# A fused cross-attention and ternary feed-forward kernel: row shifts on halves of the array, an earlier place for them in a queue, and five smaller edits

## The chip, the cores and the metric

The kernel runs on one core of one Trainium2 chip. The metric is the time of one execution in microseconds (us), as the median of several runs. TensorE (PE) multiplies, VectorE (DVE), ScalarE (ACT) and GpSimd (POOL) work on elements, and the DMA queue of SyncE (SP) moves nearly all data.

## The reference

For x of 64 batches x 64 rows x 256 and a context of 64 x 64 x 64, in float32:

```
h   = layernorm(x)                                  # 256 wide
k   = rope(ctx)                                     # kv_rope, 64 wide
q_r = h @ Wq.T, then per head @ w_kc_q @ W_qr       # 16 heads, 64 wide
k_r = k @ W_kr                                      # per head
a   = softmax(q_r . k_r)                            # over the 64 context rows
c   = a @ k;  x1 = x + (c @ w_kc_kv per head) @ Wo.T
h   = layernorm(x1)
u   = quant(rmsnorm(h)) @ ternary(w1).T             # 256 -> 1024
x2  = x1 + quant(rmsnorm(gelu(u))) @ ternary(w2).T  # 1024 -> 256
```

quant rounds a row to 8-bit steps of its own maximum; ternary rounds a weight matrix to -1, 0, 1 by its mean absolute value.

## The kernel before

**Tiling.** The 4096 rows of x are 32 tiles of 128 rows, two batches each (`NT` = 32, `LAST` = 31). The weights are folded first: `ah`/`al` hold the product that takes the normed x straight to the 16 heads' scores, `bh`/`bl` the product behind the attention; hi and lo halves keep float32 accuracy in three passes.

**Slots.** The main loop runs over slots n = 0 to 30, the same n on every engine, and a hand-written tail follows. In slot n the engines work on different stages of different tiles: scores of tile n, the exponentials of tile n, the division of tile n-2, the output projection of tile n-3, `up` (the first feed-forward matmul) of tile n-5, and `down` (the second) of tile n-7. In odd slots two tiles' `up` and two roundings of x fall due, and two tiles are normed in even ones. Every engine executes its list in the order written; semaphores tie the lists together.

**The softmax.** `quadrant_max` (DVE, two per slot) takes maxima of the scores in the PSUM banks `SB[0]`, `SB[1]`. PE turns them (`turned`, L790), and `row_max` (L1054) writes the negated maxima of a tile into `nmax`. `shift_rows` on the SP queue (L359) sends them with two small DMAs into four partitions of `shift`, which is zero elsewhere. Then `shifts` on PE adds them to the scores: two matmuls per slot (L830), one per batch, with the selecting matrix `em[:, b, :]` (128 rows by 128 columns) as stationary operand and 512 columns of `shift` as moving one. ACT takes the exponentials (L563), PE multiplies by the context (`contexts`, L838), and DVE divides (`divide`, L1074) by row sums that have gone out to DRAM (`rinv_rows`, L367) and come back spread over partitions into `rb` (`rinv_spread`, L376).

**The SP queue.** In slot n its order is: `turn_g(n-7)` (a DMA transpose of the rounded `qb`, L389), `shift_rows(n)`, `rinv_rows(n-1)`, in odd slots `turn_x` of two tiles (DMA transposes of `xq`, L381), `rinv_spread(n-1)`, in slot 1 the load of `w2`, in slot 2 a load of x, and `store(n-8)`. An instruction that waits holds up all behind it.

**DVE.** `reciprocal_deviations` makes 1/sqrt(variance) of a part of the tiles with 12 small operations that wait for one another. Parts 2 and 3 stand in slots 6 and 18 behind `g_scale`, ahead of the quadrant sums of that slot and the quadrant maxima of the next.

**Order of one slot on PE.** `scores`, then in even slots `up` of tile n-5, then `queries`, `turned` and `project` in halves, `queries`, `shifts`, in every fourth slot (2, 6, ... 26) a group of transposes `kv_t` (L744), `contexts(n-1)`, `down(n-7)`, and in odd slots `up(n-5)`. After the loop the tail has its own order.

Of the kernel before, what the change touches and what calls it, by code (L numbers as in the profile page):

```python
# [24 lines left out]
P = 128  # L25
# [9 lines left out]
BB = 4  # L35
# [15 lines left out]
RSQRT_OPS = 9  # L51
RSTD_STEPS = RSQRT_OPS + 3
# [7 lines left out]
def build(nc, x, kv, wq, wk_t, wqr, wkr_t, wkv, wo_t, w1_t, w2_t, consts, out):  # L60
    with ExitStack() as ctx:
# [16 lines left out]
        em = sb("em", [P, 2, P], F32R)  # L78
# [73 lines left out]
        cst = sb("cst", [P, 2 * DC + 3 * P], F32, at)  # L152
# [25 lines left out]
        names += """const_set shift_zeroed t_made t_copied d_made d_copied at_made at_copied a_made a_hi a_lo_done rope_steps rope_done kvt_made  # L178
# [17 lines left out]
        def rsqrt(e, v, y, a, t, out, done, n):  # L196
# [7 lines left out]
            step(e.tensor_scalar(y.bitcast(I32), v.bitcast(I32), -0.5, float(0x5F3759DF), ALU.mult, ALU.add))  # L204
            step(e.scalar_tensor_tensor(out=t, in0=v, scalar=1.0, in1=y, op0=ALU.mult, op1=ALU.mult))
            step(e.scalar_tensor_tensor(out=a, in0=t, scalar=1.0, in1=y, op0=ALU.mult, op1=ALU.mult), False)
            step(e.scalar_tensor_tensor(out=t, in0=t, scalar=1.0, in1=y, op0=ALU.mult, op1=ALU.mult))
            step(e.scalar_tensor_tensor(out=t, in0=t, scalar=-10.0 / 3.0, in1=a, op0=ALU.add, op1=ALU.mult))
            step(e.scalar_tensor_tensor(out=y, in0=t, scalar=5.0, in1=y, op0=ALU.add, op1=ALU.mult))
            step(e.scalar_tensor_tensor(out=t, in0=v, scalar=1.0, in1=y, op0=ALU.mult, op1=ALU.mult))  # L210
            step(e.scalar_tensor_tensor(out=t, in0=t, scalar=1.0, in1=y, op0=ALU.mult, op1=ALU.mult))
            step(e.scalar_tensor_tensor(out=out, in0=t, scalar=-3.0 * CUBIC * CUBIC, in1=y, op0=ALU.add, op1=ALU.mult))
            return n
# [17 lines left out]
        def reciprocal_deviations(dve, part):  # L231
# [6 lines left out]
            at_least(dve, sem["rstd_steps"], n - 1)  # L238
            if part < 2:
                dve.wait_ge(sem["bn_means"], XPARTS[part + 1])  # L240
                dve.tensor_scalar(v, mv[:, c, 1], EPS_LN, None, ALU.add).then_inc(sem["rstd_steps"], 1)
            else:
                dve.wait_ge(sem["x_sums"], 2 * (XPARTS[part + 1] - XPARTS[2]))
                dve.tensor_scalar(v, mv[:, c, 1], 1.0 / D, EPS_LN, ALU.mult, ALU.add).then_inc(sem["rstd_steps"], 1)
            dve.wait_ge(sem["rstd_steps"], n)
            n = rsqrt(dve, v, y, a, t, r, sem["rstd_steps"], n)
            dve.tensor_scalar(rstd[:, c], r, RSQRT_SCALE, None, ALU.mult).then_inc(sem["rstd_steps"], 1)
            dve.wait_ge(sem["rstd_steps"], n + 1)
            dve.scalar_tensor_tensor(out=nmean[:, c], in0=mv[:, c, 0], scalar=-1.0 if part < 2 else 1.0, in1=rstd[:, c], op0=ALU.mult, op1=ALU.mult).then_inc(sem["rstd_steps"], 1)  # L249

        cos_t = cst[:, 0:DC]
        em_c = cst[:, 2 * DC:2 * DC + 2 * P]
        id_c = cst[:, 2 * DC + 2 * P:]
# [10 lines left out]
        def tile(t):  # L264
            return 0 <= t < NT
# [53 lines left out]

        def out_tile(t):  # L320
            return (yo if t < NT - 2 else xn)[:, t % 2, :]
# [29 lines left out]
        with nc.Block() as block:  # L351
            @block.sync
            def _(sp):
                def shift_rows(u):
                    p = u % 2
                    sp.wait_ge(sem["row_maxima"], u + 1)
                    at_least(sp, sem["shifted"], 2 * (u - 1))
                    for gg in range(2):
                        sp.dma_start(shift[BB * gg:BB * gg + 2, p, :].bitcast(F32).rearrange("b (k s) -> b k s", s=32),  # L359
                                     nmax[:, p, 32 * gg:32 * gg + 32].bitcast(F32)).then_inc(sem[f"shift_rows{p}"], 16)  # L360
# [9 lines left out]
                def rinv_spread(u):  # L370
                    p = u % 2
                    sp.wait_ge(sem[f"rinv_stored{p}"], 32 * (u // 2 + 1))
                    at_least(sp, sem["ctx_divided"], 2 * u)
                    for half in range(2):
                        rows = rinv_d[p, :, :, :].rearrange("b g n -> (b g) n")[half:4 - half:3 - 2 * half, :]
                        sp.dma_start(rb[64 * half:64 * half + 64, :, :], rows.partition_broadcast(64)).then_inc(sem["rinv_spread"], 16)  # L376
# [23 lines left out]
                sp.dma_start(cst[:, 0:2 * DC + 2 * P], consts[:, 0:2 * DC + 2 * P]).then_inc(sem["consts_loaded"], 16)  # L400
# [12 lines left out]
                for n in range(LAST):  # L413
                    if tile(n - 7):
                        turn_g(n - 7)
                    shift_rows(n)
                    if tile(n - 1):
                        rinv_rows(n - 1)
                    if n % 2 and tile(n - 5):
                        turn_x(n - 5)  # L420
                        turn_x(n - 4)
                    if tile(n - 1):
                        rinv_spread(n - 1)
                    if n == 1:
                        sp.dma_start(w2_s[:, :, :], w2_t.rearrange("(a p) n -> p a n", p=P)).then_inc(sem["w2_loaded"], 16)
# [12 lines left out]
                rinv_rows(LAST)  # L438
# [23 lines left out]
            def _(pool):  # L462
# [40 lines left out]
                pool.memset(red[:, :, :], 1.0).then_inc(sem["const_set"], 2)  # L503
                pool.wait_ge(sem["rstd_steps"], RSTD_STEPS)
# [43 lines left out]
            def _(act):  # L548
# [55 lines left out]
                def w_sum(k):  # L604

                    w, s = ((w1_s, "w1_loaded"), (w2_s, "w2_loaded"))[k]
                    act.wait_ge(sem[s], 16)
# [132 lines left out]
            def _(pe):  # L740
# [84 lines left out]
                def shifts(u):  # L825
                    if u == 0:
                        pe.wait_ge(sem["shift_zeroed"], 1)
                    pe.wait_ge(sem[f"shift_rows{u % 2}"], 32 * (u // 2 + 1))
                    for b in range(2):
                        pe.matmul(SB[b], em[:, b, :], shift[:, u % 2, :], start=False, stop=True, skip_group_check=True).then_inc(sem["shifted"], 1)  # L830
# [97 lines left out]
                for q in range(4):  # L928
                    if q == 0:
                        pe.wait_ge(sem["consts_loaded"], 32)  # L930
                        pe.wait_ge(sem["const_set"], 5)
# [79 lines left out]
                down(LAST - 6)  # L1011
# [3 lines left out]
                project_high(LAST - 1)  # L1015
                up(LAST - 3, 0)
# [18 lines left out]
            def _(dve):  # L1035
                def quadrant_max(u, b):
                    if b == 0:
                        dve.wait_ge(sem["scores"], u + 1)
                        if u == 0:
                            dve.wait_ge(sem["const_set"], 5)  # L1040
# [28 lines left out]
                def divide(u, b):  # L1069
                    if b == 0:  # L1070
# [4 lines left out]
                                      rb[:, b, :].rearrange("p (h s) -> p h s", s=S), ALU.mult).then_inc(sem["ctx_divided"], 1)  # L1075
# [153 lines left out]
                dve.tensor_copy(em[:, :, :], em_c.rearrange("p (b c) -> p b c", c=P)).then_inc(sem["const_set"], 1)  # L1229
# [16 lines left out]
                for n in range(LAST):  # L1246
                    k = n // 2 + 1
                    if tile(n):
# [21 lines left out]
                    if n % 2 == 0 and tile(n - 6):  # L1270
# [3 lines left out]
                        if n in (6, 18):  # L1274
                            reciprocal_deviations(dve, 2 + n // 18)
# [115 lines left out]
```

## Time and profile before

| | |
|---|---|
| time before, median of 3 runs | 413.43 us (412.06 to 414.34) |
| profiled execution, its time | 413.87 us |
| profiled execution, its span | 412.1 us |
| granted TensorE clock, mean | 0.996 |
| busy: PE, DVE, ACT, POOL | 90%, 76%, 67%, 52% |
| main loop, slots 4 to 29 | about 73 to 354 us of the span |

A row of a timeline gives start, length, engine, line of the kernel, operation, operands, number of instructions, and in brackets the idle time of the engine ahead of it with what ended it. Matmuls overlap in time: a float32r matmul of 256 columns is shown with 0.28 us, and the next starts 0.12 us after it. "SPq" is the issue of a DMA by SyncE, not its transfer.

### The profile page before, as it was taken

How to read it: one execution, taken by the hardware profiler on the slowest of the kernel's cores; microseconds unless marked ns; L12 is line 12 of the kernel's file. 1: busy time of each engine (PE TensorE's matmuls, PEld its weight loads, DVE VectorE, ACT ScalarE, POOL GpSimd, SP SyncE). 2: the span in 40 equal slices, each digit the busy share in tenths (PEclk: the TensorE clock that was granted, in tenths of full speed). 3: DMA queues.
4: the chain of work that ended last, by engine and by line, in shares of the span. 5: the costliest groups of instructions: out<-in, count | busy, mean ns of one | idle time of the engine just before them, and what ended most of it. 6: DMA issues, size and time to landing. Idle time of an engine off the chain costs nothing.

```text
span 412.1 us, 8855 instructions
## 1 busy us (share of the span) xinstructions
PE 371.6 (90%) x2829; PEld 267.3 (65%) x2829; DVE 312.0 (76%) x859; ACT 276.8 (67%) x541; POOL 215.6 (52%) x262
## 2 busy tenths in 40 slices
PE   0978879999899999999999999999999999886775
PEld 0657547667677776767676767777777767544632
DVE  0497656687978687868787988868787878796884
ACT  1253467799786888878777768585848585855771
POOL 1120132792738375756666563827382746594770
PEclk9999998999999999999999999999999999999999
DMA  8999055313344435442525335252444353434446
GB/s 272 365 431 295 18 156 155 79 45 91 46 86 92 106 90 105 92 104 71 123 71 112 84 68 127 42 131 60 109 82 104 93 105 91 105 93 104 103 111 120
DMA packets 63901, 48.81 MB, mean 118 GB/s; under 512 B 50160, under 2 KB 55536, under 8 KB 62704
## 3 DMA queue, kind: packets, MB, share of 16 engines
q1 hardware_dynamic: 63328, 45.50, 45.0%
q10 hardware_dynamic: 528, 2.75, 2.0%
q8 instruction: 23, 0.38, 0.4%
q14 instruction: 22, 0.18, 0.2%
HBM read 31.98 MB, written 4.46 MB: 88 GB/s over the span
## 4 chain that ended last, share of the span: by engine, by line
issue 29%; POOL 26%; PE 20%; DMA 10%; DVE 7%; SPq 4%; ACT 2%; POOLq 1%; ACTq 0%; DVEq 0%
POOL tq L489 6%; POOL cl L466 6%; POOL qb L492 6%; DMA cst<-consts 4%; POOL xa L479 2%; POOL xn L331 2%; PE hps L775 2%; DMA shift<-nmax 2%; PE ps L757 2%; POOL yc L474 2%; PE ps L838 2%; PE ps L759 2%; PE ps L758 2%; DMA qt<-qb 2%; PE hps L848 2%
## 5 line engine op out<-in xcount | busy, mean ns | idle before, releaser
L466 POOL TENSOR_TENSOR cl<-cr,ch 128x512 fp32r<-128x512 f32 x63 | 79.3, 1280 | 111.0 <-ACT ch L568 111.0
L757 PE MATMUL ps<-xh,ah 128*128 128x256 f32 x256 | 74.9, 292 | 1.3 <-DVE xl L348 0.8
L552 ACT ACTIVATE qf<-ps 128x512 f32<-128x512 f32 x64 | 38.0, 594 | 53.8 <-PE ps L759 53.8
L758 PE MATMUL ps<-xl,ah 128*128 128x256 f32 x256 | 71.4, 279 | 0.0
L759 PE MATMUL ps<-xh,al 128*128 128x256 f32 x256 | 71.4, 279 | 0.0
L848 PE MATMUL hps<-bh,ch 128*128 128x256 f32 x232 | 68.5, 295 | 0.0
L850 PE MATMUL hps<-bh,cl 128*128 128x256 f32 x232 | 64.6, 279 | 0.0
L849 PE MATMUL hps<-bl,ch 128*128 128x256 f32 x232 | 64.5, 278 | 0.0
L757 PEld LDWEIGHTS ps<-xh,ah 128*128 128x128 f32 x256 | 48.4, 189 | 16.5 <-issue 15.2
L1041 DVE TRANSPOSE_TENSOR_REDUCE red<-hps 128x16 f32<-128x512 f32 x64 | 41.5, 686 | 19.9 <-PE hps L775 19.9
L568 ACT ACTIVATE ch<-cr 128x512 fp32r<-128x512 f32 x64 | 37.9, 625 | 24.3 <-DVE cr L1074 24.3
L1048 DVE TRANSPOSE_TENSOR_REDUCE red<-pe 128x16 f32<-128x512 f32 x64 | 41.7, 688 | 12.0 <-ACT pe L563 11.8
L584 ACT ACTIVATE g<-ps,scl 128x512 f32<-128x512 f32 x64 | 40.7, 684 | 14.0 <-PE ps L870 13.8
L758 PEld LDWEIGHTS ps<-xl,ah 128*128 128x128 f32 x256 | 48.1, 188 | 0.0
L759 PEld LDWEIGHTS ps<-xh,al 128*128 128x128 f32 x256 | 48.1, 188 | 0.0
L848 PEld LDWEIGHTS hps<-bh,ch 128*128 128x128 f32 x232 | 43.6, 188 | 3.2 <-issue 1.6
L849 PEld LDWEIGHTS hps<-bl,ch 128*128 128x128 f32 x232 | 43.6, 188 | 0.3
L1074 DVE TENSOR_TENSOR cr<-ps,rb 128x512 f32<-128x512 f32 x64 | 41.2, 685 | 3.3 <-DMA rb<-rinv_d 2.7
L850 PEld LDWEIGHTS hps<-bh,cl 128*128 128x128 f32 x232 | 43.5, 187 | 0.0
L563 ACT ACTIVATE pe<-hps 128x512 f32<-128x512 f32 x64 | 34.6, 596 | 6.7 <-PE hps L830 6.6
L331 POOL TENSOR_SCALAR xn<-xs,rstd,nmean 128x256 f32<-128x256 f32 x32 | 18.6, 595 | 37.3 <-DVE nmean L249 30.0
L870 PE MATMUL ps<-w1q,xqt 128*128 128x512 bf16 x128 | 33.5, 380 | 5.0 <-DMA xqt<-xq 4.1
(185 smaller groups left out, 815.6 us busy)
## 6 DMA issues: line engine op xcount, KB each, us to landing
rb<-rinv_d SPq DMA_DIRECT2D x64, 256.0 KB, 4.1
out<-yo SPq DMA_DIRECT2D x30, 128.0 KB, 3.8
wo_s<-wo_t SPq DMA_DIRECT2D x1, 2048.0 KB, 17.6
xs<-x SPq DMA_DIRECT2D x2, 1024.0 KB, 10.9
w_s<-w_t SPq DMA_DIRECT2D x2, 1024.0 KB, 11.6
xs<-x SPq DMA_DIRECT2D x1, 1536.0 KB, 20.9
wk_a<-wk_t ACTq DMA_DIRECT2D x1, 1024.0 KB, 6.3
wq_s<-wq ACTq DMA_DIRECT2D x1, 1024.0 KB, 13.3
```

What stands on the lines that cost most here:

```text
L466: pool.tensor_tensor(cl[:, u % 2, :, b * S:(b + 1) * S], cr[:, :, b * S:(b + 1) * S], ch[:, u % 2, :, b * S:(b + 1) * S].bitcast(F32), ALU ...
L552: act.activation(qf[:, k % 2, 2 * b:2 * b + 2, :], turn_bank("q", k, b).rearrange("p (h t) -> p h t", t=TB), ACT.Copy).then_inc(sem["q_cop ...
L584: act.activation(g[:, t % GB, 512 * half:512 * half + 512], turn_bank("h", t, half), ACT.Gelu, scale=hscale(scl, t)).then_inc(sem["gelu_do ...
L757: pe.matmul(o, ah[:, c, cols], xh[:, k % 2, c, :], start=(c == 0), stop=False)
L758: pe.matmul(o, ah[:, c, cols], xl[:, k % 2, c, :], start=False, stop=False)
L759: m = pe.matmul(o, al[:, c, cols], xh[:, k % 2, c, :], start=False, stop=(c == KC - 1))
L848: pe.matmul(O[:, 0:D], c_h, bh[:, hp, :], start=(hp == 0), stop=False)
L849: pe.matmul(O[:, 0:D], c_h, bl[:, hp, :], start=False, stop=False)
L850: m = pe.matmul(O[:, 0:D], c_l, bh[:, hp, :], start=False, stop=(hp == HP - 1))
L1041: dve.tensor_reduce(red[:, u % 2, 16 * b:16 * b + 16], SB[b].rearrange("p (k s) -> p k s", s=32), AX.X, ALU.max, apply_transpose=True).the ...
L1048: dve.tensor_reduce(red[:, (u + 1) % 2, 64 + 16 * b:80 + 16 * b], pe32[:, u % 2, b, :].rearrange("p (k s) -> p k s", s=32), AX.X, ALU.add, ...
L1074: dve.tensor_tensor(cr[:, :, b * S:(b + 1) * S], CB[b].rearrange("p (h s) -> p h s", s=S), rb[:, b, :].rearrange("p (h s) -> p h s", s=S), ...
```

## The change

1. `shifts`: the two matmuls of a slot now use 64 rows each. `em` becomes one 128 x 128 matrix with four ones rows, at partitions 0, 32, 64 and 96; batch b takes partitions 64b to 64b+63 of `em` and of `shift`. The four rows of `shift` lie at these partitions.
2. `em` is written by POOL (one memset of 128 x 128 and four of one row) ahead of all its other work; DVE's copy of it and 128 KB of the load of constants go.
3. SP queue: in odd slots `shift_rows(n)` stands ahead of `turn_g(n-7)`; in even slots nothing changes.
4. `reciprocal_deviations` of part 2 is split: its first 6 operations at the start of slot 8, its last 6 at the start of slot 10; part 3 the same at slots 16 and 18. Both stand ahead of that slot's quadrant maxima.
5. `w2` is loaded in two halves, behind `shift_rows` of slots 0 and 1, no longer in one piece behind `rinv_spread(0)`.
6. Last tile: its spread row sums go to a free part of `qf`, so `rinv_spread(31)` waits for the scores of tile 30 and no longer for the division of tile 30.
7. Tail: `turn_x(27)` and `x_round(27)` come earlier, `turn_g(24)`, `turn_g(25)`, `g_round(25)` and `down(25)` later.

```
     def shift_rows(u): ...
-            sp.dma_start(shift[BB * gg:BB * gg + 2, p, :]...
+            sp.dma_start(shift[32 * gg:32 * gg + 65:64, p, :]...
     def rinv_spread(u): ...
-        at_least(sp, sem["ctx_divided"], 2 * u)
+        if u < LAST:
+            at_least(sp, sem["ctx_divided"], 2 * u)
+        else:
+            sp.wait_ge(sem["scores"], u - 1)
...
     for n in range(LAST):                      # SP
+        if n % 2:
+            shift_rows(n)
         if tile(n - 7):
             turn_g(n - 7)
-        shift_rows(n)
+        if n % 2 == 0:
+            shift_rows(n)
+        if n in (0, 1):
+            sp.dma_start(w2_s[:, 4 * n:4 * n + 4, :], ...).then_inc(sem["w2_loaded"], 16)
         if tile(n - 1):
             rinv_rows(n - 1)
...
     shift_rows(LAST)                           # SP, tail
     turn_x(LAST - 5)
+    turn_x(LAST - 4)
+    rinv_rows(LAST - 1)
     turn_g(LAST - 7)
-    rinv_rows(LAST - 1)
+    rinv_spread(LAST - 1)
+    rinv_rows(LAST)
     turn_g(LAST - 6)
-    rinv_spread(LAST - 1)
-    turn_x(LAST - 4)
-    rinv_rows(LAST)
     rinv_spread(LAST)
...
     g_round(LAST - 7)                          # POOL, tail
     x_round(LAST - 5)
-    g_round(LAST - 6)
+    x_round(LAST - 4)
     ctx_lo(LAST - 2, 0)
     ctx_lo(LAST - 2, 1)
-    x_round(LAST - 4)
     centre(LAST - 3)
+    g_round(LAST - 6)
     centre(LAST - 2)
...
     for b in range(2):                         # PE, shifts
-        pe.matmul(SB[b], em[:, b, :], shift[:, u % 2, :], start=False, stop=True, ...)
+        rows = slice(64 * b, 64 * b + 64)
+        pe.matmul(SB[b], em[rows, :], shift[rows, u % 2, :], start=False, stop=True, ...)
...
     down(LAST - 7)                             # PE, tail
-    down(LAST - 6)
     up(LAST - 4, 0)
     up(LAST - 4, 1)
     contexts(LAST)
     project_high(LAST - 1)
+    down(LAST - 6)
...
     for n in range(LAST):                      # DVE
+        if n in (8, 16):
+            reciprocal_deviations(dve, 1 + n // 8, True, False)
+        if n in (10, 18):
+            reciprocal_deviations(dve, 1 + n // 9, False, True)
...
-            if n in (6, 18):
-                reciprocal_deviations(dve, 2 + n // 18)
```

## Rows read from the trace of the kernel before

**Rows 1.** The page: busy time, share of the span and instructions of each engine.

```profile
PE 371.6 (90%) x2829; PEld 267.3 (65%) x2829; DVE 312.0 (76%) x859; ACT 276.8 (67%) x541; POOL 215.6 (52%) x262
```

**Rows 2.** Waits of PE, 64 to 363 us: total, times, longest.

```profile
PE hps L830 <- DMA shift<-nmax: 4.6, 5, 1.5
PE hps L790 <- DVE red L1041: 2.7, 3, 1.4
```

**Rows 3.** Windows: length, busy times of engines, granted clock, DMA share, GB/s.

```profile
60.90:64.30 3.40, 3.40 (x18) 1.58 (x20) 2.00 (x3) 3.06 (x5) 1.04 (x2) 0.50 0.52 125
```

**Rows 4.** Timeline of PE, slot 15: the shifts and what follows.

```profile
198.34 0.64 PE L830 MATMUL hps<-shift,em 128*128 128x512 f32 x2
198.91 0.64 PE L838 MATMUL ps<-pe,kvn 64*64 64x512 f32 x1
...
199.39 0.59 PE L838 MATMUL ps<-pe,kvn 64*64 64x512 f32 x1
...
199.93 1.05 PE L891 MATMUL hps<-w2q,qt 128*128 128x256 bf16 x8
```

**Rows 5.** Timeline of DVE, slots 6 and 16: deviations and quadrant maxima.

```profile
102.06 0.17 DVE L244 TENSOR_SCALAR hps<-mv 128x8 f32<-128x8 f32 x1
...
104.28 1.29 DVE L1048 TRANSPOSE_TENSOR_REDUCE red<-pe 128x16 f32<-128x512 f32 x2
...
202.93 1.31 DVE L1041 TRANSPOSE_TENSOR_REDUCE red<-hps 128x16 f32<-128x512 f32 x2 [1.05 <-PE hps L775]
```

**Rows 6.** Timeline of PE, slot 7: the turn of the maxima.

```profile
106.82 0.33 PE L790 MATMUL hps<-ident,red 128*128 128x128 f32 x1 [1.40 <-DVE red L1041]
```

**Rows 7.** Timelines of DVE, SP and PE, slot 13.

```profile
171.89 0.28 DVE L1054 TENSOR_REDUCE nmax<-hps 32x64 fp32r<-32x128 f32 x1
...
172.28 1.88 SPq L389 DMA_TRANSPOSE qt<-qb  x1
174.25 1.40 SPq L359 DMA_DIRECT2D shift<-nmax  x2
...
176.66 2.48 SPq L381 DMA_TRANSPOSE xqt<-xq  x2
...
176.81 0.73 PE L830 MATMUL hps<-shift,em 128*128 128x512 f32 x2 [0.72 <-DMA shift<-nmax]
...
178.49 1.05 PE L891 MATMUL hps<-w2q,qt 128*128 128x256 bf16 x8
179.37 1.03 PE L870 MATMUL ps<-w1q,xqt 128*128 128x512 bf16 x4
```

**Rows 8.** DMA issues: the last number is us to landing.

```profile
xqt<-xq SPq DMA_TRANSPOSE x32, 2.3
qt<-qb SPq DMA_TRANSPOSE x32, 3.5
```

**Rows 9.** Timelines of SP, PE and DVE, slot 2.

```profile
53.20 0.58 SPq L425 DMA_DIRECT2D w_s<-w_t  x1
...
56.04 1.36 SPq L359 DMA_DIRECT2D shift<-nmax  x2
...
60.52 0.91 PE L830 MATMUL hps<-shift,em 128*128 128x512 f32 x2 [2.23 <-DMA shift<-nmax]
...
63.44 0.69 DVE L1216 TENSOR_TENSOR bl<-hps,bh 128x512 fp32r<-128x512 f32 x1 [0.44 <-ACT bh L629]
```

**Rows 10.** Chain that ended last, and timelines of DVE and SP, the tail.

```profile
371.16 3.32 DMA rinv_d<-ri
...
379.49 1.29 DVE L1074 TENSOR_TENSOR cr<-ps,rb 128x512 f32<-128x512 f32 x2 [2.71 <-DMA rb<-rinv_d]
...
380.85 1.25 SPq L376 DMA_DIRECT2D rb<-rinv_d  x2
...
385.73 1.29 DVE L1074 TENSOR_TENSOR cr<-ps,rb 128x512 f32<-128x512 f32 x2
```

**Rows 11.** Timeline of DVE, the start: the copy of em.

```profile
19.76 0.29 DVE L1229 CAST em<-cst 128x256 fp32r<-128x256 f32 x1
```

More of the change, by code:

```diff
@@ L194, in at_least, with rsqrt @@
                 e.wait_ge(s, value)
-        def rsqrt(e, v, y, a, t, out, done, n):
+        def rsqrt(e, v, y, a, t, out, done, n, begin=True, end=True):
             def step(ins, wait=True):
@@ L229, in statistics, with reciprocal_deviations @@
                     dve.bn_aggr(mv[:, t - 1, :], st6[:, (t - 1) % 4, :]).then_inc(sem["bn_means"], 1)
-        def reciprocal_deviations(dve, part):
+        def reciprocal_deviations(dve, part, begin=True, end=True):
             c = slice(XPARTS[part], XPARTS[part + 1])
@@ L237, in reciprocal_deviations @@
             n = part * RSTD_STEPS + 1
[L238 to L241, printed above, removed]
-            else:
[L243 to L249, printed above, removed]
+            if begin:
+                at_least(dve, sem["rstd_steps"], n - 1)
+                if part < 2:
+                    dve.wait_ge(sem["bn_means"], XPARTS[part + 1])
+                    dve.tensor_scalar(v, mv[:, c, 1], EPS_LN, None, ALU.add).then_inc(sem["rstd_steps"], 1)
+                else:
+                    dve.wait_ge(sem["x_sums"], 2 * (XPARTS[part + 1] - XPARTS[2]))
+                    dve.tensor_scalar(v, mv[:, c, 1], 1.0 / D, EPS_LN, ALU.mult, ALU.add).then_inc(sem["rstd_steps"], 1)
+                dve.wait_ge(sem["rstd_steps"], n)
+                n = rsqrt(dve, v, y, a, t, r, sem["rstd_steps"], n, True, end)
+            else:
+                n = rsqrt(dve, v, y, a, t, r, sem["rstd_steps"], n + RSQRT_BEGIN, False, True)
+            if end:
+                dve.tensor_scalar(rstd[:, c], r, RSQRT_SCALE, None, ALU.mult).then_inc(sem["rstd_steps"], 1)
+                dve.wait_ge(sem["rstd_steps"], n + 1)
+                dve.scalar_tensor_tensor(out=nmean[:, c], in0=mv[:, c, 0], scalar=-1.0 if part < 2 else 1.0, in1=rstd[:, c], op0=ALU.mult, op1=ALU.mult).then_inc(sem["rstd_steps"], 1)
         cos_t = cst[:, 0:DC]
-        em_c = cst[:, 2 * DC:2 * DC + 2 * P]
-        id_c = cst[:, 2 * DC + 2 * P:]
+        id_c = cst[:, 2 * DC:]
         hd = DC // 2
@@ L372, in rinv_spread @@
                     sp.wait_ge(sem[f"rinv_stored{p}"], 32 * (u // 2 + 1))
-                    at_least(sp, sem["ctx_divided"], 2 * u)
+                    if u < LAST:
+                        at_least(sp, sem["ctx_divided"], 2 * u)
+                    else:
+                        sp.wait_ge(sem["scores"], u - 1)
                     for half in range(2):
                         rows = rinv_d[p, :, :, :].rearrange("b g n -> (b g) n")[half:4 - half:3 - 2 * half, :]
-                        sp.dma_start(rb[64 * half:64 * half + 64, :, :], rows.partition_broadcast(64)).then_inc(sem["rinv_spread"], 16)
+                        sp.dma_start(spread_rows(u)[64 * half:64 * half + 64, :, :], rows.partition_broadcast(64)).then_inc(sem["rinv_spread"], 16)
                 def turn_x(t):
@@ L503, in _ @@
                 pool.memset(red[:, :, :], 1.0).then_inc(sem["const_set"], 2)
+                pool.memset(em[:, :].bitcast(F32), 0.0).then_inc(sem["em_set"], 1)
+                pool.wait_ge(sem["em_set"], 1)
+                for d in range(2):
+                    for b in range(2):
+                        row = 64 * b + 32 * d
+                        pool.memset(em[row:row + 1, 64 * d:64 * d + 64].bitcast(F32), 1.0).then_inc(sem["em_set"], 1)
+                pool.wait_ge(sem["em_set"], 5)
                 pool.wait_ge(sem["rstd_steps"], RSTD_STEPS)
@@ L827, in shifts @@
                         pe.wait_ge(sem["shift_zeroed"], 1)
+                        pe.wait_ge(sem["em_set"], 5)
                     pe.wait_ge(sem[f"shift_rows{u % 2}"], 32 * (u // 2 + 1))
                     for b in range(2):
-                        pe.matmul(SB[b], em[:, b, :], shift[:, u % 2, :], start=False, stop=True, skip_group_check=True).then_inc(sem["shifted"], 1)
+                        rows = slice(64 * b, 64 * b + 64)
+                        pe.matmul(SB[b], em[rows, :], shift[rows, u % 2, :], start=False, stop=True, skip_group_check=True).then_inc(sem["shifted"], 1)
                 def contexts(u):
```

45 lines of the change are left out of this document (24 added, 21 removed).

## The prediction, written before the changed kernel ran

> **What bounds the kernel now.** I read the page's busy times first, then the waits of PE, then the timelines of single slots on all engines, and the chain of waits for the tail alone. PE is busy for 371.6 of 412.1 us [rows 1], so the reader should ask of every edit whether it takes something off PE's own list of work or out of its few gaps. The waits of PE over the main loop name just two gaps of size: 4.6 us for the shift rows' DMA, in 5 places, and 2.7 us for DVE's quadrant maxima, in 3 places [rows 2]. The longest of the first (1.5) is slot 30's; the other four are 0.7 to 0.9 us each, in slots 9, 13, 21 and 25 (slot 13: [rows 7]). Ahead of the loop's steady part one gap of 2.23 us stands in slot 2 [rows 9]; behind it PE runs at half clock for 3.4 us [rows 3], the one place in the loop where the granted clock falls (1.2 for 2.4 GHz). The tail is another regime: there PE waits often, and the chain of waits runs through DMA and POOL, so it must be followed by due times, not by PE's work.
>
> **The pair of shifts.** Before, slot 15 has the pair start at 198.34 and the contexts at 198.91: 0.57 us [rows 4]. The pair's row is 0.64 long and one such matmul is shown with 0.40, so the second starts 0.24 after the first, and 0.33 remain to the contexts. The contexts run on quarters of the array (64*64), four at once: one set starts 0.48 after the other, and the next full-array work 0.54 after the second set [rows 4]. Their 64 x 512 float32 pass needs some 0.43, which I take from the difference: so about 0.05 is added by a first set whose weights aren't loaded ahead, about 0.1 by leaving a mode, and by the 0.33 against 0.24 above about 0.1 by entering one. Two half-array matmuls on different rows and into different banks should run at once, as the four quarters do. The new pair then costs 0.1 to enter, 0.21 for 512 columns (0.24 less 0.03 of overhead), 0.05 for its weights and 0.11 to leave: 0.48 against 0.57, a gain of 0.09, not of 0.24. The bounds: 0.24 gained if nothing is paid for the modes; 0.14 lost if the halves run one after the other (0.48 + 0.24 - 0.57, rounded down). I take 0.08, since entering and leaving are in the same rows. In the seven slots with L744 behind the pair a switch more is paid, and I count nothing. In slots 0, 1, 2, 30 and 31 the exponentials follow the first matmul alone, so nothing is won either.
>
> The Trainium skill (TensorEngine Tiling (Array Packing), Tiling Modes, key properties) says that changing the tiling mode, not just the tile, drains the engine. By its speedup for a contraction of 64 or less alone (up to 2x, same page) 31 pairs would give 31 x 0.24 = 7.4 us; with the drain the rows' prices leave 31 x 0.08 = 2.5 at most, and the 0.1 us on either side of the contexts agree with the drain.
>
> **The shift ahead of turning g, odd slots.** Slot 13 [rows 7]: the maxima are ready at 172.17. SP has begun to issue the turning of g at 172.28 and takes 1.88 us, so the shift's two issues go out from 174.25 to 175.65 and PE starts the pair at 176.81, 1.16 after. After the change they go out from 172.2 to 173.6, and land at 174.8, before PE comes (176.81 - 0.72, or 176.1). The wait goes whole: 0.72 idle, some 0.16 more that the last matmul's shown length hides, and 0.1 since a pair after a wait has its weights loaded late. That is 1.0 us. What is late next: down(6) wants qt at 178.49 - 1.0 = 177.5; issued at 173.7 it lands 3.5 later [rows 8], at 177.2, with 0.3 to spare. up(8) started at 179.37; its xqt was issued at 176.66 and landed 2.3 later [rows 8], 178.96, so it had 0.4 in hand. SP's list between the maxima and that issue keeps its length: only the 0.1 us between 172.17 and 172.28 goes. So turned x comes 0.1 earlier, PE 1.0 earlier, and 0.5 is what slot 13 really gains. The same in slots 9, 21 and 25: 4 x 0.5 = 2.0, between 1.0 (a late qt as well) and 4.0 (turned x not the limit). Slot 17 has a smaller wait of the kind: 0.3. In slots 11, 15, 23 and 27, where PE didn't wait, the queue is now 0.25 later at turned x, with 0.1 to 0.4 in hand: about 0.1 lost in each, 0.4 in all. Behind the moved turn_g stand rinv_rows, two turn_x and rinv_spread; the divisions that need the last come a slot later.
>
> **Small pairs.** Nine slots without L744 and without these limits (3, 5, and 4, 8, ... 28) gain 0.08 each, 0.7; with the 0.4 lost above, 0.3.
>
> **Deviations in two parts.** In slot 6 the block runs from 102.06 to 104.28, 2.22 us on DVE, and the quadrant sums and maxima stand behind it [rows 5]. PE's turn of slot 7 waits 1.40 [rows 6]; slot 19 has 0.89 of the kind, part of the 2.7 [rows 2]. Each half is some 1.1 us, and DVE sits idle ahead of the quadrant maxima in even slots: 1.05 in slot 16 [rows 5], 1.26 to 1.43 in slots 8, 10 and 18. So they are hidden, up to 0.1 in slot 16; without that cover they would cost 1.1 each. With the maxima on time the small shift waits of slots 7 and 19 go too (0.3 each). Slot 7 gains 1.6 and slot 19 1.2: 2.8, between 2.0 and 3.3.
>
> **Second weight in halves.** Slot 2: w2's megabyte goes out at 53.20, the shift rows at 56.04 to 57.40, and PE gets them at 60.52, 3.1 after the issue and not 1.16 as in slot 13 [rows 9, 7]. After, half of it goes out at 42 and half at 50. The shift then lands at 58.6 to 59.0. But the second half now stands ahead of rinv_rows(0) and rinv_spread(0), and the shift rows of slot 2 behind that spread; division(0) comes up to 2 us later, ctx_hi and a query copy behind it on ACT, and the exponentials end about when they did. Then b_lo(3), at 63.44 to 64.13 [rows 9], holds PE's queries of slot 3, which started at 65.1: the gain is about 1.2. Bounds: 0.5, and 2.23 + 1.7 (half of the 3.4 at half clock) = 3.9 if DVE and ACT follow.
>
> **Start.** em's copy on DVE goes: 0.2 us from its start to that of the next operation [rows 11], on a chain of DVE work that leads without a gap to the first queries. 128 KB less in the load before it may give 0.2 more. POOL's five memsets stand where it waits 15 us. I take 0.4, between 0.2 and 0.6.
>
> **Tail.** Three things go by due times. rinv_rows(30) took 3.32 us to land, among two turnings of g [rows 10]; now rinv_spread(30) can go out at about 373.5 and not at 374.5, and division(30) starts at 378.0, not 379.49. rinv_spread(31) waited until 380.85, just behind division(30) [rows 10]; with its own buffer it goes out at 378, and division(31) waits no longer for it but for DVE's list: 384.2, not 385.73. up(28) waited for its x behind that spread: it comes 2.5 earlier. Behind them POOL's list is shorter by a wait of 1.3 for a turned x. From there all stands in series (g_round, turn_g, down). I take 2.0, between 0.5 (a moved turn_g(24) or down(25) late) and 3.0.
>
> **Sum.** 0.4 + 1.2 + 2.8 + 2.3 + 0.3 + 2.0 = 9.0 us. From the profiled execution, 413.87, this gives 404.9; the runs' median is 0.44 lower, so 404.4.
>
> **Rivals.**
> (a) The halves run one after the other. Against it: four quarters start within 0.03 us. Then 24 pairs cost 0.14 more instead of 0.7 us gained in all: -9.0 + 0.7 + 3.4 = -4.9, 408.5.
> (b) The SP queue takes back what PE's gaps give: turned x holds PE in all odd slots (0.4 in hand [rows 7, 8]). Then the four slots and slot 17 give nothing (2.3), slots 7 and 19 half (1.4), and in the tail a late turned g leaves 0.5: -9.0 + 2.3 + 1.4 + 1.5 = -3.8, 409.6.
> (c) Slower. Each half-array pair waits for the whole length of the matmul ahead, and runs in turn: 0.16 (0.28 less 0.12) to enter, 0.24 + 0.40, 0.16 + 0.11 to leave, 1.07 against 0.57. 31 x 0.5 = 15.5 against 8.7 of other gains: 420. It decides from 0.3 us per pair. For it: no row has this shape with 512 columns. Against it: the contexts' mode costs 0.1 on each side.
> (d) All waits are returned whole: four slots 3.8, slot 2 2.9, tail 2.5: 413.4 - 13.3 = 400.
>
> **Chances.** Forecast 0.62, (a) 0.15, (b) 0.10, (c) 0.04, (d) 0.09. The forecast's own range is 401 to 408. The range for 8 in 10 is 400 to 409.5: it takes in (a) and most of (d), and leaves out (c) and part of (b). About 0.5%, 2 us, is what a measurement tells from no change. Faster 0.92, within 0.5% 0.04, slower 0.04.
>
> **What would show it.** The pair's two rows start within 0.05 us of each other, and 0.45 to 0.5 us lie between its start and the contexts. The waits of L830 for the DMA stay in slots 0, 30 and 31 only, but waits of L870 for xqt appear in odd slots; if these reach 0.5 in more than four slots, (b) is right. L790's waits shrink to slot 29's 0.4. Slot 2 keeps a gap under 0.8 at L830, and the half clock goes. The last tile's division starts 1.5 us earlier against scores(31). I am wrong if the pair takes over 0.6, or if turned g holds down in odd slots.

## The result and the profile after

The changed kernel takes 407.5 us (median of 4 runs, 406.43 to 408.71), the kernel before 413.08 in the same session (4 runs, 412.06 to 414.34). The ratio is 0.9864, with a 95% interval from 0.9824 to 0.9904. Forecast were 404.4, between 400.0 and 409.5. So the sign and the range hold; 3.1 us of the forecast gain are missing. By its number alone the result lies nearer to rival (a)'s 408.5 than to the forecast, though (a)'s mechanism isn't what happened (see the pair, below). The profiled execution of after took 408.71 us (span 407.1), the slowest of its four, 5.16 less than that of before (413.87), where 9.0 had been forecast.

The page's busy times, to be held against [rows 1], and the granted clock in 40 slices:

```profile
PE 372.9 (92%) x2813; PEld 266.5 (65%) x2829; DVE 310.9 (76%) x858; ACT 275.6 (68%) x541; POOL 215.3 (53%) x267
...
PEclk9989998999999999999999999999999999997998
```

PE's busy time did not fall though its shift pairs are shorter (0.51 us in slot 13 below, for 0.64 in [rows 4]). The granted clock is part of that: before, its row had one slice under 9, in slot 2; here slices at the start, in slot 2 and twice in the tail are slower. The waits of PE in the loop, 64 to 355 us, where [rows 2] had 4.6 and 2.7 us:

```profile
PE hps L854 <- DMA shift<-nmax: 1.6, 1, 1.6
...
PE hps L812 <- DVE red L1065: 0.4, 1, 0.4
...
PE ps L894 <- DMA xqt<-xq: 0.3, 1, 0.3
```

The shift waits of slots 9, 13, 21 and 25 are gone, slot 30's stays; the turned maxima wait in slot 29 alone. No wait for turned x of size has come in their place. I split the profiled difference by the start of scores(n), which begins a slot, and use this accounting all through:

```
                          before   after   gained   forecast
to scores(2)               52.82   52.38    0.44      0.4
slots 2 and 3              20.55   20.53    0.02      1.2
slot 7                     12.53   10.77    1.76      1.6
slot 19                    12.11   10.83    1.28      1.2
slots 9, 13, 21, 25        47.67   43.29    4.38      2.0
slot 17                    11.25   10.75    0.50      0.3
all other slots                            -0.32      0.3
scores(31) to last down    45.22   48.12   -2.90      2.0
sum                                         5.16      9.0
```

Slot 13 of after, timelines of SP and PE, answers [rows 7]:

```profile
168.99 1.12 SPq L368 DMA_DIRECT2D shift<-nmax  x2
170.22 1.29 SPq L401 DMA_TRANSPOSE qt<-qb  x1
171.60 0.98 SPq L376 DMA_DIRECT2D rinv_d<-ri  x2
172.68 2.46 SPq L393 DMA_TRANSPOSE xqt<-xq  x2
...
172.78 0.51 PE L854 MATMUL hps<-shift,em 64*128 64x512 f32 x2
173.22 0.64 PE L862 MATMUL ps<-pe,kvn 64*64 64x512 f32 x1
...
174.24 1.05 PE L915 MATMUL hps<-w2q,qt 128*128 128x256 bf16 x8
```

PE comes to the shift without a wait. The shift's issue takes 1.12 us, not 1.40, and turning g 1.29, not 1.88. Counted from the maxima's end, turned x is issued at 3.7 us (172.68 - 168.96) and not at 4.5 (176.66 - 172.17). That leaves PE its whole microsecond here, where the forecast took 0.5. The pair's contexts follow 0.44 after its start; from the last matmul ahead of the pair (172.58) to the contexts it is 0.64.

Slot 2 of after, timelines of PE, DVE and SP, answers [rows 9]:

```profile
59.06 0.50 PE L854 MATMUL hps<-shift,em 64*128 64x512 f32 x2 [1.20 <-DMA shift<-nmax]
...
60.90 1.08 PE L862 MATMUL ps<-pe,kvn 64*64 64x512 f32 x1 [0.75 <-DVE cr L1098]
...
59.47 1.29 DVE L1098 TENSOR_TENSOR cr<-ps,rb 128x512 f32<-128x512 f32 x2 [2.99 <-DMA rb<-rinv_d]
...
49.48 0.42 SPq L433 DMA_DIRECT2D w_s<-w_t  x1
49.94 0.97 SPq L376 DMA_DIRECT2D rinv_d<-ri  x2
53.74 2.07 SPq L388 DMA_DIRECT2D rb<-rinv_d  x2
```

One gap of 2.23 became two, 1.20 and 0.75. The second is new: w2's second half now goes out ahead of rinv_rows(0) and its spread, the first division starts at 59.47 (56.95 before), and the contexts wait for it.

The tail of after, timelines of SP, DVE and PE, answers [rows 10]:

```profile
362.81 1.00 SPq L376 DMA_DIRECT2D rinv_d<-ri  x2
363.90 1.82 SPq L401 DMA_TRANSPOSE qt<-qb  x1
366.59 1.29 SPq L388 DMA_DIRECT2D rb<-rinv_d  x2
...
371.55 1.29 DVE L1098 TENSOR_TENSOR cr<-ps,rb 128x512 f32<-128x512 f32 x2 [2.45 <-DMA rb<-rinv_d]
...
377.62 1.29 DVE L1098 TENSOR_TENSOR cr<-ps,qf 128x512 f32<-128x512 f32 x2
...
369.50 0.59 PE L894 MATMUL ps<-w1q,xqt 128*128 128x512 bf16 x2 [0.75 <-ACT g L606]
372.98 1.08 PE L862 MATMUL ps<-pe,kvn 64*64 64x512 f32 x1 [2.89 <-DVE cr L1098]
```

Against scores(31), division(30) stands at +16.49 (before +16.37) and division(31) at +22.56 (+22.61): neither came the 1.5 us earlier that the forecast had counted on. The windows of after (columns as in [rows 3]) hold the rest:

```profile
60.90:64.30 3.40, 3.35 (x16) 0.61 (x16) 1.72 (x3) 3.40 (x7) 3.40 (x4) 0.50 0.58 154
371.50:378.30 6.80, 5.32 (x24) 3.74 (x24) 6.34 (x21) 3.53 (x6) 3.02 (x3) 0.50 0.48 103
398.80:402.20 3.40, 3.40 (x10) 1.22 (x8) 0.77 (x2) 0.12 (x1) 0.00 (x0) 0.50 0.62 152
```

Clock 0.50 is 1.2 GHz. Before had one such stretch in the loop and none in the tail; after has the same one, 10.2 us in the tail, and one of 3.4 us at the start (19.9 to 23.3).

### The profile page after: what moved, and what is told of

Same layout as the page of the kernel before. It is cut to its first block, busy times and chain, and to the rows that moved or that the text cites. A ratio compares the mean times of both kernels' runs of the same rounds, so it can differ in the third digit from the quotient of the medians.

```text
span 407.1 us, 8847 instructions
## 1 busy us (share of the span) xinstructions
PE 372.9 (92%) x2813; PEld 266.5 (65%) x2829; DVE 310.9 (76%) x858; ACT 275.6 (68%) x541; POOL 215.3 (53%) x267
## 4 chain that ended last, share of the span: by engine, by line
issue 37%; POOL 35%; PE 9%; DMA 7%; DVE 6%; ACT 2%; SPq 2%; POOLq 1%; ACTq 0%; DVEq 0%
POOL tq L504 8%; POOL cl L481 8%; POOL qb L507 7%; DMA cst<-consts 4%; POOL xa L494 4%; POOL yc L489 3%; POOL xn L340 3%; POOL xq L497 2%; PE hps L797 1%; DMA rb<-rinv_d 1%; PE ps L779 1%; DMA qt<-qb 1%; PE ps L781 1%; ACT pe L585 1%; PE ps L780 1%
## 5 line engine op out<-in xcount | busy, mean ns | idle before, releaser
L1098 DVE TENSOR_TENSOR cr<-ps,rb 128x512 f32<-128x512 f32 x62 | 39.9, 685 | 8.0 <-DMA rb<-rinv_d 7.6
L862 PE MATMUL ps<-pe,kvn 64*64 64x512 f32 x128 | 36.4, 643 | 3.6 <-DVE cr L1098 3.6
L1127 DVE TENSOR_REDUCE amax<-g 128x1 f32<-128x1024 f32 x32 | 37.6, 1211 | 0.0
L340 POOL TENSOR_SCALAR xn<-xs,rstd,nmean 128x256 f32<-128x256 f32 x32 | 17.5, 557 | 37.3 <-DVE nmean L256 29.5
## 6 DMA issues: line engine op xcount, KB each, us to landing
kv_s<-kv SPq DMA_DIRECT2D x1, 1024.0 KB, 14.9
```

What stands on the lines that cost most here:

```text
L1098: dve.tensor_tensor(cr[:, :, b * S:(b + 1) * S], CB[b].rearrange("p (h s) -> p h s", s=S), spread_rows(u)[:, b, :].rearrange("p (h s) -> p ...
```

## Experiments

Twelve kernels ran, in three sessions of four, each beside the kernel before on the same chip (medians of before: 413.11, 412.64, 413.07). "Loop" is scores(0) to scores(31) of the profiled execution, 326.0 us before.

**1. Half-array pair alone.**

```diff
-  sp.dma_start(shift[BB * gg:BB * gg + 2, p, :] ...
+  sp.dma_start(shift[32 * gg:32 * gg + 65:64, p, :] ...
-  pe.matmul(SB[b], em[:, b, :], shift[:, u % 2, :], ...)
+  pe.matmul(SB[b], em[rows, :], shift[rows, u % 2, :], ...)   # rows: 64 of each b
```

`em` is written by POOL here and in 2 (edit 2 of the change), since its ones stand in other rows.

> Before, with the half-array pair of shift matmuls and the shift rows at partitions 0, 32, 64 and 96 alone. Theory: the changed kernel's pair gives 0.05 us in the slots without L744 and costs 0.05 in those with it, so the pair itself is worth 0.5 to 1.0 us; the shift rows' two DMAs take 1.12 us to issue and not 1.39, so the four slots that wait for them (9, 13, 21, 25) wait 0.2 to 0.3 us less each, 1.0 more: 411.3. The rival, that the shorter issue in the changed kernel came from the order of SP's list and not from where the rows land: issues stay at 1.39 and only the pair is left, 412.4. The recorded rival of halves that run one after the other would give 416.

Measured: 410.44 us (10 runs), ratio 0.9939 [0.9904, 0.9974]; loop 320.8. That is faster than either expectation.

**2. The rows 32 partitions apart, full-array matmuls.** As 1, but em keeps its two planes of 128 rows and the matmul its full form.

> Before, with the shift rows at partitions 0, 32, 64 and 96, but the two matmuls still over the full array. Theory: issue of the two DMAs 1.12 us for 1.39, four waiting slots 0.2 to 0.3 us shorter each, pair unchanged at 0.57 to the contexts: 412.1. Rival: where the rows land has no effect on the issue, 413.1; then all that the first of these kernels gains is the array mode's.

Measured: 409.22 us (4 runs), ratio 0.9896 [0.9833, 0.996]; loop 321.3; faster than either expectation again. So what experiment 1 gains doesn't come from half the array: that adds 0.5 us in the profile and nothing in the medians. In both, the two issues take 1.12 to 1.15 us for 1.36 to 1.40. They also gained 2.2 us in slots 2 and 3 (18.3 for 20.55): a shift wait of 1.2 and no half clock, with w2 whole. That isn't the rows' doing: experiment 9, with the rows side by side, takes 18.52 there, and experiment 10, with the rows apart and w2 whole, 20.70. Of slots 9, 13, 21 and 25, two (9 and 21) lost the whole wait at once, since turning g took 1.3 us there, and two (13 and 25) kept a part, with turning g at 1.8 to 2.2. Even this is in part the luck of one execution: experiments 4 and 5, which change nothing in slot 9, gained 0.63 us there, each with a short turning of g.

**3. The order alone.**

```diff
+                    if n % 2:
+                        shift_rows(n)
                     if tile(n - 7):
                         turn_g(n - 7)
-                    shift_rows(n)
+                    if n % 2 == 0:
+                        shift_rows(n)
```

> Before, with only the shift's DMAs ahead of turning g in odd slots. Theory: the waits of slots 9, 13, 21 and 25 go (0.7 to 0.9 each, 1.0 with what the last matmul hides), but with issues of 1.39 us turned x comes later than in the changed kernel by 0.27, so 0.7 to 1.0 of it stays gained: 3.4 us in all, 409.7, and PE shows waits for turned x up to 0.3 in these slots; SP's turning of g takes 1.3 us in them and not 1.9, since it is no longer issued while PE's instructions are fetched. The forecast's step (turned x allows 0.5 a slot, with turning of g as long as before): 2.0 us, 411.1.

Measured: 409.28 us (5 runs), ratio 0.9892 [0.9823, 0.9961]; slots 9, 13, 21 and 25 gained 0.93, 0.88, 1.02 and 0.90, slot 17 0.28; slot 19 lost 0.88. The forecast's 0.5 a slot falls with the old issues too. The timeline of its SP in slot 13:

```profile
171.73 1.36 SPq L359 DMA_DIRECT2D shift<-nmax  x2
173.19 1.29 SPq L389 DMA_TRANSPOSE qt<-qb  x1
```

Behind the shift, turning g takes 1.29 again. The DMA view of the moment of the long one, before, 172.28 to 174.16 us (packets, MB, share of 16 engines), and of the short one of after, 170.22 to 171.51:

```profile
q1 hardware_dynamic: 483, 0.12, 49.7%
q8 instruction: 1, 0.02, 3.2%
```

```profile
q1 hardware_dynamic: 86, 0.01, 6.1%
```

The long issue has a fetch of instructions beside it and eight times the other traffic (share 49.7% for 6.1%); in after that fetch falls into the shift's issue, which is not longer for it (1.12). All four long ones of before (129, 173, 260, 304 us) have a fetch beside them. But the fetch alone does not do it, against what was expected here: in experiment 4 the same turning of g at 173 us has the fetch and takes 1.28, after has two of 1.29 with it (192 and 276 us), and in experiment 8 one of 2.22 (360 us) has none. What makes the issue long stays open.

**4. The deviations alone.**

```diff
+                    if n in (8, 16):
+                        reciprocal_deviations(dve, 1 + n // 8, True, False)
+                    if n in (10, 18):
+                        reciprocal_deviations(dve, 1 + n // 9, False, True)
-                        if n in (6, 18):
-                            reciprocal_deviations(dve, 2 + n // 18)
```

> Before, with only the deviations in two parts. Theory (as forecast, and as the loop of the changed kernel showed: 1.76 us in slot 7, 1.29 in slot 19): 2.8 to 3.0 us in the loop, 410.2. Rival: part of it is won only together with the shift ahead of turning g, since PE comes to slots 7 and 19 earlier and then waits for the shift rows' DMA: 2.2, 410.9.

Measured: 412.86 us (10 runs), ratio 0.9991 [0.9953, 1.0029]. Both expectations fell, though the rival had named the mechanism; the edit is worth nothing by itself. The timelines of DVE, SP and PE in its slot 7:

```profile
106.92 0.28 DVE L1061 TENSOR_REDUCE nmax<-hps 32x64 fp32r<-32x128 f32 x1 [0.49 <-PE hps L797]
...
108.19 1.27 SPq L396 DMA_TRANSPOSE qt<-qb  x1
109.57 1.39 SPq L366 DMA_DIRECT2D shift<-nmax  x2
...
112.17 0.73 PE L837 MATMUL hps<-shift,em 128*128 128x512 f32 x2 [1.05 <-DMA shift<-nmax]
...
115.69 0.59 PE L877 MATMUL ps<-w1q,xqt 128*128 128x512 bf16 x2 [0.80 <-DMA xqt<-xq]
```

The maxima are ready at 107.20, but SP's list has turning g first, and that waits for POOL's rounding until 108.16. The shift leaves at 109.57, and PE waits 1.05 for it and 0.80 for turned x behind it.

**5. w2 in halves alone.**

```diff
+                    if n in (0, 1):
+                        sp.dma_start(w2_s[:, 4 * n:4 * n + 4, :], ...)
                     if tile(n - 1):
                         rinv_rows(n - 1)
...
-                    if n == 1:
-                        sp.dma_start(w2_s[:, :, :], ...)
```

> Before, with only the second weight in halves. Theory: its second half goes out ahead of rinv_spread(0), so rb(0) lands some 2.5 us later, the first division with it, and the contexts of slot 2 wait for that division (0.75 us in the changed kernel) besides what is left of the wait for the shift (1.2): two gaps close together for one of 2.23, the half clock in slot 3 as before, and no gain: 412.6 to 413.3. The forecast's step: 1.2 us gained, 411.9.

Measured: 414.26 us (10 runs), ratio 1.0039 [1.0004, 1.0073]: by itself this part makes the kernel 1.6 us slower, just clear of no change, and both expectations fell. Its profiled execution, the slowest of the ten (417.21), does not show the loss at its place: slots 2 and 3 take 20.30 us there (20.55 before), with gaps of 1.28, 0.37, 0.94 and 0.61 us and no half clock, while scores(0) comes 0.95 later and the tail is 1.9 longer.

**6. Changed kernel, tail lists of before.** In SP's, POOL's and PE's lists behind slot 31, turning and rounding of g of tile 25 and down(25) go back ahead of what had been put before them.

> The changed kernel, with SP's, POOL's and PE's lists behind slot 31 in the order of before (the buffer of its own for the last spread rows stays). Theory: the tail lost 2.9 us because down(25) no longer stands ahead of contexts(31), so that PE has a longer gap there (2.9 us), and 6.8 us at half clock behind it. With the old lists scores(31) to the last down takes 45 to 46 us again and not 48: 2.0 to 2.9 less, 405.0. Rival: the longer tail came from the loop's own changes (rows of slots 28 to 30 late), and the lists have no part in it: 407.5.

Measured: 405.85 us (4 runs), ratio 0.9851 [0.9775, 0.9927]. Its profiled execution is the slowest of the four (410.24): it had half clock for 10.2 us in the tail, as after has, behind gaps of 1.73 and 1.55 and later of 2.22 us, and lost 3.5 us in slots 23 and 24, with half clock for 3.4 more. The old lists don't keep the clock up. Slots 2 and 3 had no half clock in this execution and still took 20.34 us. PE's waits from 54 to 66 us:

```profile
PE hps L854 <- DMA shift<-nmax: 1.2, 1, 1.2
PE hps L797 <- ACT pe L585: 0.9, 1, 0.9
PE ps L779 <- DVE bl L1240: 0.6, 1, 0.6
PE ps L862 <- DVE cr L1098: 0.5, 1, 0.5
```

Two of the four are for what comes behind the late division: the exponentials, 0.9, and the division itself, 0.5.

**7. Changed kernel, late filler.**

```diff
                 up(LAST - 4, 1)
+                keep_clock(SB[1], 12)    # behind the waits that down(25) has
                 contexts(LAST)
```

> The changed kernel, with 12 filler matmuls (2.6 us at full clock) in the gap ahead of contexts(31), waiting as down(25) does before. Theory: the granted clock stays at full there, contexts(31) takes 1.0 and not 1.9 us and project_high(30) 1.9 and not 3.4; the chain then waits for rb(31) and DVE, so of these 2.4 us about 1.5 reach the end: 406.0. Rival: the order of the due times on SP and POOL costs the 2.9 us, not the clock: clock full, yet 407.5.

Measured: 405.35 us (4 runs), ratio 0.9807 [0.9742, 0.9872]. The clock had fallen before the filler began and was back before contexts(31), which took 1.0 and project_high(30) 1.9. From scores(30) to the last down it took 55.3 us for after's 57.1, though the filler held contexts(31) up by 1.8 (it starts 3.2 us behind division(30), for 1.4 in after) and slot 30 had a stretch of half clock of its own.

**8. Changed kernel, w2's second half behind rinv_spread(0).**

```diff
-                    if n in (0, 1):
+                    if n == 0:
...
                     if tile(n - 1):
                         rinv_spread(n - 1)
+                    if n == 1:
+                        sp.dma_start(w2_s[:, 4:8, :], ...)
```

> The changed kernel, with the second half of w2 moved behind rinv_spread(0) (the first stays where it is). Theory: rb(0) lands 2.5 us earlier, the contexts of slot 2 no longer wait for the first division, and one gap of about 1.2 us is left, after which the clock stays full, as in the two kernels with the shift rows 32 partitions apart and w2 whole (scores(2) to scores(4) 2.2 us shorter): 2.0 less, 405.5. Rival: the clock falls there all the same, since the gap at the shift stays 1.2: 0.7 less, 406.8.

Measured: 403.16 us (4 runs), ratio 0.9758 [0.9689, 0.9826]; slots 2 and 3 take 17.57 us. Timelines of its SP and DVE, to be held against slot 2 of after:

```profile
50.83 1.32 SPq L388 DMA_DIRECT2D rb<-rinv_d  x2
52.20 0.58 SPq L442 DMA_DIRECT2D w_s<-w_t  x1
55.10 1.13 SPq L368 DMA_DIRECT2D shift<-nmax  x2
...
56.00 1.29 DVE L1100 TENSOR_TENSOR cr<-ps,rb 128x512 f32<-128x512 f32 x2
```

And PE's waits from 54 to 66 us, all there are:

```profile
PE ps L781 <- DVE bl L1242: 0.6, 1, 0.6
```

The spread is 2.9 us earlier and the division doesn't wait. Ahead of the shift rows the queue has half a megabyte and not a whole one as before; that half lands at 59.09, yet the pair starts at 57.36 without a wait (60.52 before, with the whole load). So even that wait is gone, which is more than the theory (2.0) gave. Experiments 11 and 12, with the same list, take 17.56 in these slots.

**9. Order and deviations together.** The edits of 3 and 4.

> Before, with the shift ahead of turning g in odd slots and the deviations in two parts together. Alone, the order took 2.4 us off the loop and the deviations none (maxima of slot 6 to those of slot 8: 22.24 us before, 22.23 with the order, 22.44 with the deviations, 20.49 in the changed kernel). Theory: each needs the other in slots 7 and 19, since without the new order turning g stands ahead of the shift there, and without the divided deviations DVE's maxima are late. Together 2.4 + 1.75 + 1.3 = 5.4 us in the loop, 407.4. Rival: the gain of slots 7 and 19 came from the shorter shift of the half arrays, and they stay as they are: 410.

Measured: 407.05 us (4 runs), ratio 0.984 [0.9811, 0.987]. Slots 7 and 19 take 10.97 and 10.98 us (12.53 and 12.11 before; 10.77 and 10.83 after). These two parts give all that the whole change gives. That doesn't make the rest worth nothing: experiment 10, in the same session, is the whole change without the halves of w2 and takes 404.25.

**10. Changed kernel, w2 whole.** The load of before in its old place, the rest as changed.

> The changed kernel, with the second weight loaded whole behind rinv_spread(0), as before. Theory: its halves took 2 us from what the rest had made possible; as in the two kernels with the rows 32 partitions apart, one gap of 1.2 and no half clock stand in slot 2, scores(2) to scores(3) is 8.6 and not 10.55: 405.5. With the first half early and only the second behind the spread it was 7.6, so the order of merit is: second half late, whole, halves as in the change. Rival: the halves as such are needed for the 7.6, and the whole load brings back the half clock: 407.5.

Measured: 404.25 us (4 runs: 402.71, 403.10, 405.40, 405.77), ratio 0.9779 [0.974, 0.9819]. The time is as expected, the mechanism isn't: its profiled run, the slowest, had a wait of 2.44 for the shift and the half clock, and slots 2 and 3 took 20.70. Its mean granted clock was 0.992, as in the other slow run; the two quicker runs had 1.000, so no half clock anywhere. They have no profile of their own.

**11. As 8, with the tail lists of before.**

> The changed kernel with the second half of w2 behind rinv_spread(0), and with the tail's lists of before. The tail, from scores(30) to the last down, took 54.3 us before, 57.1 in the changed kernel, 55.6 with the old lists and 55.0 with the new lists where the first slots were faster. Theory: where the clock falls in the tail hangs on gaps of 2.5 to 3 us that either list has, and the lists themselves are worth under 0.5: 403.2 like the new lists. Rival: the new lists cost 1.5 to 2 us whenever they run: 401.5.

Measured: 403.13 us (4 runs), ratio 0.9755 [0.9727, 0.9783], against 0.9758 with the new lists: no difference. All four runs lie above the rival's 401.5.

**12. As 8, with two early fillers.**

```diff
-                down(LAST - 7)
+                down(LAST - 7, 6)
                 up(LAST - 4, 0)
                 up(LAST - 4, 1)
+                keep_clock(SB[1], 8)
                 contexts(LAST)
```

> The changed kernel with the second half of w2 behind rinv_spread(0) and with filler matmuls in the two gaps ahead of contexts(31): 6 ahead of down(24) (a gap of 1.7 us), 8 behind up(27) (2.7). Theory: the gaps are what makes the clock fall; with them filled early it stays full from down(24) to the end of project_high(30), contexts(31) takes 1.0 and not 1.9 us, project_high(30) 1.9 and not 2.4: 1.0 to 1.5 less than without fillers, 402.0. Rival: what follows waits for rb(31) and DVE, so the end stays: 403.2.

Measured: 401.87 us (4 runs, 400.68 to 403.03), ratio 0.9722 [0.9693, 0.975], the fastest of all. Its PE around the two gaps, and the window from there to the end of the work:

```profile
363.25 1.46 PE L847 MATMUL hps<-w1q 128*128 128x512 bf16 x6
365.19 1.05 PE L917 MATMUL hps<-w2q,qt 128*128 128x256 bf16 x8 [0.48 <-DMA qt<-qb]
...
366.94 1.89 PE L847 MATMUL hps<-w1q 128*128 128x512 bf16 x8
369.68 0.61 PE L864 MATMUL ps<-pe,kvn 64*64 64x512 f32 x1 [0.86 <-DVE cr L1101]
```

```profile
362.00:400.50 38.50, 28.71 (x180) 17.45 (x182) 28.18 (x92) 20.88 (x39) 19.65 (x23) 1.00 0.54 117
```

The granted clock is 1.00 throughout, and the tail 44.5 us. The intervals of 11 and 12 overlap, so the fillers' own 1.3 us is likely, not shown; and the fastest of the four runs (400.68) had a mean clock of 0.990, so a full clock is not what made it fast.

## Why the forecast held, and where it failed

**Tail (forecast 2.0, measured -2.9).** This is the step that failed, in both its halves. First the due times: "now rinv_spread(30) can go out at about 373.5 and not at 374.5, and division(30) starts at 378.0". Against scores(31) the spread went out at +11.53, and +10.4 would have been the forecast (before: +11.38); rinv_rows(30) still took 3.2 us to land, for 3.3, with one turning of g beside it instead of two, and the spread then landed 4.9 after its issue, as before. And "with its own buffer it goes out at 378 ...: 384.2, not 385.73": the forecast meant +14.9, but the spread went out at +16.89 (before +17.72), when rinv_rows(31) had landed, 3.4 us after its issue. It landed 0.77 us ahead of division(31), but DVE had the maxima of g in front (2.33 us from 374.94), so the own buffer bought nothing here. Then the clock, which the forecast had left out of the tail. All the traces, from scores(30) to the last down, with the time at half clock in between (experiment in brackets):

```
old lists:  54.3 (before)  0     54.0 (3)  0     53.8 (2)  3.4    54.0 (4)  3.4
            53.2 (11)  3.4       56.2 (5)  6.8   54.9 (1)  6.8    55.6 (6) 10.2    56.9 (9) 10.2
new lists:  54.2 (10)  3.4       55.0 (8)  6.8   57.1 (after) 10.2
fillers:    55.3 (7)  6.8        53.2 (12) 0
```

The order of the tail's work makes no difference that these show. The three with 10.2 us at half clock took 55.6 to 57.1, those with 6.8 took 54.9 to 56.2, those with 3.4 or none 53.2 to 54.3. An estimate from the times and mean clocks of all 110 executions of the experiments, after and before: within one kernel, 1 us more at half clock goes with 0.18 us more time (standard error 0.04), so 10.2 us with 1.9. So a good part of the 2.9 us goes with the clock of one execution; whether the clock or the gaps come first these numbers don't say, and the rest of the 2.9 stays open. What the lists themselves give is about 0, not 2.0. My theory at experiment 6, that the moved down(25) opened the gap that costs them, falls: the old lists had the same stretches there, and in experiment 11 the same time.

**Slot 2 (forecast 1.2, measured 0.0).** The forecast named the delay ("division(0) comes up to 2 us later"), and sent its effect through the exponentials. It missed that PE's own contexts wait for that division (0.75), and the exponentials did end later (0.9 in experiment 6). Its sign for slot 2, a gap under 0.8 at the shift and no half clock, failed with 1.20 and the half clock. Experiments 8 and 10 show the price: taking the halves back from the changed kernel wins (ratio 0.978 for 0.986); moving only the second half past the spread takes 3.0 us off slots 2 and 3, in three traces. The half clock is not the price itself: with the halves as changed and without it, experiments 6 and 7 still took 20.34 and 19.57 us. The 1.6 us that the halves lose alone (5) its trace doesn't place. The forecast's upper bound was 3.9, "if DVE and ACT follow"; 3.0 was there to be had, by a change that wasn't made.

**Odd slots (forecast 2.3, measured 4.9).** The mechanism is right and the term mis-sized. "SP's list between the maxima and that issue keeps its length" failed: it lost 0.28 (1.40 to 1.12) from where the shift rows land and 0.6 (1.88 to 1.29) from turning g, whose long issue went with the place it had in these four slots. Of the two it is turning g that counts: experiment 3, with the shift issue still at 1.36, gained 0.9 a slot. Turned x held PE once in the loop, for 0.3. For these four slots rival (d), which gave all waits back (3.8), was nearer than the forecast's 2.0: measured are 4.4.

**Deviations (2.8, measured 3.04).** Right in size, but booked wrongly as a part of its own. Experiment 4 gives nothing in slots 7 and 19 (-0.2 and -0.1), nor does experiment 3 (-0.1 and -0.9), and 9 gives both (1.6 and 1.1): DVE and SP each ended the same wait. The forecast came out because both edits were in the change.

**The pair (0.08 a slot, measured 0.05 or -0.1).** Rival (a) and rival (c) are out: the row of both matmuls is 0.51 us long in slot 13, so they run at once. But from the last matmul ahead to the pair's start it is 0.21 us where it was 0.12, against 0.43 for 0.56 from there to the contexts; in slots with the transposes of L766 behind the pair, 0.1 is lost. The 0.1 that slots 11, 15, 23 and 27 were to lose to a later turned x didn't come (0.02 to 0.07 gained). The Trainium skill (TensorE: Matmul & The Clock Gate, the table row on small-K matmuls) has matmuls on separate row groups start within 4 ns of each other; this trace agrees (3 ns between the two). What is won so is mostly paid back on entering the mode.

**Start (0.4, measured 0.44).** The size is right by luck in this pair of executions. scores(0) came only 0.04 earlier, at 37.06, and 0.4 was gained in slots 0 and 1. But after ran at half clock from 19.9 to 23.3, as did experiment 11 (scores(0) at 36.90). In the seven other traces with the new `em` scores(0) stands at 36.23 to 36.56, in the five with the old one (before, 3, 4, 5, 9) at 36.85 to 38.05. So the forecast's 0.4 is there, and hidden in after.

In sum: +2.6 in the odd slots and +0.2 in the deviations against -1.2 in slot 2, -0.6 in the small pairs and -4.9 in the tail, or 5.2 for 9.0. That the time fell within the range is in part luck: the loop gave 2.8 us more than forecast in two terms, and this covers part of the 6.7 missing in the three others.

## What to carry to other kernels

When two engines are both late at one wait, neither edit shows anything alone (none in slots 7 and 19, 2.7 us together in experiment 9), so ask of each wait what is late next before booking a gain. Of a bulk load that is cut up and moved forward, follow each small DMA that it now stands ahead of, to the last reader on the busiest engine; here one place in the list moved the ratio from 0.986 to 0.976. In a tail with gaps, look at the granted clock of several executions before crediting or blaming an order of work.

## What the runs showed of the hardware

- **The clock after a gap isn't set by the gap alone.** In after, 2.89 us of idle ahead of contexts(31) went with half clock. With the order alone (experiment 3) PE was idle for 2.82 us at the same time of the tail, ahead of up(27), and the clock stayed full:

```profile
371.00:378.00 7.00, 4.06 (x27) 1.00 0.45 109
```

  In slot 2 gaps of 2.23, 2.68 and 2.44 us were followed by half clock, as were 1.20 and 0.75 together, while 1.63 with 2.03 a slot later (experiment 4) was not, nor 1.20 and 0.54 together (experiment 6). The Trainium skill (TensorE: Matmul & The Clock Gate, Part 1) says that the number of slowed matmuls at the start of one and the same kernel varies from run to run. No run here counts them; in the middle of a kernel these traces vary too: of the three with the same list in slot 2 (after, experiments 6 and 7) one has half clock there.
- **The issue of a small DMA depends on the partitions it writes:** 1.36 to 1.40 us for two to rows side by side, 1.12 to 1.15 to rows 64 apart, each of the same 4 KB.
- **Turning g was issued mostly in 1.2 to 1.3 us, and at times in up to 2.6,** at other places from one execution to the next. A fetch of instructions stands beside many of the long ones, but beside short ones as well, and some long ones have none; the cause is open.
